# Two-layer graph network: summing each PSUM bank by itself, and a correction computed on GpSimd

## The reference

```python
# layer 0
h = jnp.maximum(_layernorm(x), 0.0)
mask = (adj > 0.0).astype(x.dtype)
W1a, W1b = W1[:F], W1[F:]                     # F = 64, H = 192
diff = h[:, :, None, :] - h[:, None, :, :]
hid = relu((h @ W1a)[:, :, None, :] + diff @ W1b + b1)
hm = jnp.einsum('bjkh,bjk->bjh', hid, mask)
x = x + hm @ W2 + deg[..., None] * b2
# layer 1
h = jnp.maximum(_layernorm(x), 0.0)
x = x + jnp.einsum('bno,fo->bnf', jnp.einsum('bnm,bmf->bnf', adj, h), W)
```

## Time and profile before

| | |
|---|---|
| median of three runs | 945.11 us (942.63 to 945.84) |
| the profiled execution, its own time | 940.0 us |
| its span, first to last instruction | 938.2 us |
| granted TensorE clock, mean | 0.989 |
| busy: PE, DVE, ACT, POOL | 889.5, 885.7, 832.2, 582.1 us |
| matmuls, DVE, ACT, POOL instructions | 9138, 3032, 1856, 1420 |

### The profile page before, as it was taken

The page is one execution under the profiler, slowest core; times in us unless marked ns, Lnnn a source line. Parts: engine busy times, 40 slices in busy tenths (PEclk is TensorE's granted clock), DMA queues, the critical chain, the costliest instruction groups (busy, mean ns, idle before and its releaser), DMA issues.

```text
span 938.2 us, 28102 instructions
## 1 busy us (share of the span) xinstructions
PE 889.5 (95%) x9138; PEld 818.6 (87%) x9139; DVE 885.7 (94%) x3032; ACT 832.2 (89%) x1856; POOL 582.1 (62%) x1420
## 2 busy tenths in 40 slices
PE   3879999999999999999999999999999999999996
PEld 1459999999999999999999999999999999999995
DVE  6999999999999999999999999999999999999993
ACT  3978999999999999999999999999999999899993
POOL 0856666666666665666666665666666666656664
PEclk9799999999999999999999999999999999999998
DMA  9500000000000000000000000000000000000000
GB/s 340 223 1 2 7 8 2 8 8 7 8 7 8 7 2 8 7 7 8 8 7 2 8 8 6 9 8 6 2 7 8 7 8 9 7 5 4 8 7 15
DMA packets 8114, 19.18 MB, mean 20 GB/s; under 512 B 1312, under 2 KB 5920, under 8 KB 6944
## 3 DMA queue, kind: packets, MB, share of 16 engines
q1 hardware_dynamic: 7056, 16.98, 4.8%
q10 hardware_dynamic: 912, 0.39, 0.2%
HBM read 13.17 MB, written 4.19 MB: 19 GB/s over the span
## 4 chain that ended last, share of the span: by engine, by line
PE 64%; DVE 25%; ACT 4%; issue 4%; POOL 1%; DMA 1%; DVEq 0%; SPq 0%; ACTq 0%; POOLq 0%
PE ring L353 31%; DVE acc L745 13%; PE post L438 8%; PE ring L379 5%; DVE onehot_space L729 5%; PE post L439 4%; ACT ring L502 3%; PE prep L409 3%; PE post L442 2%; PE prep L419 2%; PE prep L416 2%; PE prep L415 2%; DVE onehot_row L781 2%; DVE owner L775 1%; DMA x_all<-x_nbf_dram 1%
## 5 line engine op out<-in xcount | busy, mean ns | idle before, releaser
L502 ACT COPY ring<-P 128x768 f32<-128x768 f32 x512 | 405.2, 814 | 44.0 <-DVE acc L745 35.1
L353 PE MATMUL ring<-PQ,onehot_space 128*128 128x192 f16 x4096 | 401.0, 246 | 18.1 <-ACT ring L502 14.6
L353 PEld LDWEIGHTS ring<-PQ,onehot_space 128*128 128x128 f16 x4096 | 341.1, 99 | 29.8 <-DVE onehot_space L729 17.1
L745 DVE SCALAR_TENSOR_TENSOR acc<-ring,acc 128x768 f32<-128x768 f32 x384 | 362.2, 943 | 0.7 <-PE ring L353 0.7
L828 POOL TENSOR_TENSOR relu_row<-relu_row 128x192 f32<-128x192 f32 x256 | 154.4, 603 | 255.5 <-ACT relu_row L538 245.5
L729 DVE TENSOR_SCALAR onehot_space<-mask_all 128x256 f16<-128x256 f16 x1024 | 230.4, 266 | 0.0
L438 PE MATMUL post<-consts,acc 128*128 128x128 f32 x1024 | 154.4, 273 | 1.5 <-POOL relu_row L828 1.5
L745 DVE SCALAR_TENSOR_TENSOR acc<-ring,start 128x768 f32<-128x768 f32 x128 | 121.7, 951 | 28.3 <-PE ring L353 28.1
L438 PEld LDWEIGHTS post<-consts,acc 128*128 128x128 f32 x1024 | 114.2, 141 | 1.6 <-issue 1.6
L439 PE MATMUL post<-ownerT,relu_row 128*128 128x128 f32 x512 | 99.0, 275 | 0.0
L379 PE MATMUL ring<-PQ,owner 128*128 128x384 f16 (+1 forms) x512 | 93.9, 306 | 0.0
(11 more groups left out here) (129 smaller groups left out, 1609.1 us busy)
## 6 DMA issues: line engine op xcount, KB each, us to landing
adj_all<-adj_kbj_dram SPq DMA_DIRECT2D x8, 1024.0 KB, 17.9
x_all<-x_nbf_dram SPq DMA_DIRECT2D x8, 512.0 KB, 18.6
out_dram<-x_all SPq DMA_DIRECT2D x32, 128.0 KB, 1.7
consts<-consts_dram SPq DMA_DIRECT2D x1, 192.0 KB, 2.6
onehot_space<-w1a_dram ACTq DMA_DIRECT2D x2, 48.0 KB, 4.2
onehot_space<-w1b_dram ACTq DMA_DIRECT2D x2, 48.0 KB, 6.9
onehot_space<-b_dram ACTq DMA_DIRECT2D x1, 96.0 KB, 9.8
w2a<-w_dram ACTq DMA_DIRECT2D x1, 32.0 KB, 11.3
```

Source lines behind the costliest of these rows:

```text
L353: last = nc.tensor.matmul(to, hot(s), parts[:, part, H:2 * H], start=False, stop=(part == 1), skip_group_check=True)
L502: return nc.scalar.copy(slots[to], src.unsqueeze(1).unsqueeze(1).broadcast_to([N, BANKS, PER_BANK, H]))
L745: return nc.vector.scalar_tensor_tensor(sums, slots[to], 0.0, so_far, ALU.max, ALU.subtract if first else ALU.add)
```

## The change

Each sum instruction takes one PSUM bank (384 columns), so that both banks are added into one running sum of two slots (384 columns) and only two slots for each half k have to be transposed: 4 transposes a graph instead of 8. PE signals after each bank's gather (9 signals a graph instead of 5). DVE runs 8 half sums instead of 4 sums; the second half of a chunk waits for the first, and the second of two compares moves between the two halves. The correction `start` is no longer halved, and POOL makes it from the copy of P in SBUF, behind `p_ready` and the graph's first sum, in front of L851; ACT no longer makes it. What waited for `start_ready` to know that ACT had read `pq_ps` now waits for `p_ready`. (The kernel has a second form of the loop for graphs whose extra rows don't fit; its changes are left out here.)

```diff
-        acc_space = sb("acc", [N, 2, BANKS * ROW + N - H2])
-        acc = acc_space[:, :, 0:BANKS * ROW].rearrange("p g (a w) -> p g a w", a=BANKS)
+        acc_space = sb("acc", [N, 2, ROW + N - H2])
+        acc = acc_space[:, :, 0:ROW].rearrange("p g (s h) -> p g s h", h=H)
...
-                            dst = [slot(place(u, i), s) for s in range(SLOTS)]
                             hot = lambda s: onehot[:, hot_place(u // 2, i), s, u % 2, :]
                             pe.wait_ge(seeded, b * REGULAR + i + 1)
+                            for bank_ in range(BANKS):
+                                dst = [(s, slot(place(u, i), s)) for s in range(PER_BANK * bank_, PER_BANK * (bank_ + 1))]
+                                gather(dst, parts, hot).then_inc(gathered, 1)
...
                             for k in range(2):
-                                for s in range(SLOTS):
+                                for s in range(PER_BANK):
                                     hm = acc_space[:, (u + 1) % 2, s * H + k * N:s * H + (k + 1) * N]
                                     nc.tensor.matmul(sums_T_ps[:, k, :], hm, ident, start=(s == 0), stop=False, is_transpose=True)
...
-            def start_sums(b):
-
-                nc.scalar.activation(start[:, 0, :], pq_ps[:, 0:H], ACT.Relu, scale=spare[:, bass.ds(b, 1)]).then_inc(start_ready, 1)
...
-            def prepare(b, u, i):
+            def prepare(b, u, i, s):
...
-            def consume(u, to, first):
-
-                sums = acc[:, u % 2].rearrange("p a (s h) -> p a s h", h=H)
-                so_far = start[:, :, :].unsqueeze(1).broadcast_to([N, BANKS, PER_BANK, H]) if first else sums
-                return nc.vector.scalar_tensor_tensor(sums, slots[to], 0.0, so_far, ALU.max, ALU.subtract if first else ALU.add)
+            def consume(u, to, bank_, first):
+
+                sums = acc[:, u % 2]
+                return nc.vector.scalar_tensor_tensor(sums, slots[to][:, bank_], 0.0, start[:, :, :] if first else sums, ALU.max,
+                                                      ALU.subtract if first else ALU.add)
...
                     if i < REGULAR:
-                        prepare(b, u, i)
+                        prepare(b, u, i, 0)
                     if i == 3 and main and exists(b + 1):
-                        dve.wait_ge(start_ready, b + 2)
+                        dve.wait_ge(p_ready, b + 2)
                         second_part(b + 1, u + 1)
...
-                        dve.wait_ge(gathered, b * CHUNKS + i + 1)
-                        consume(u, place(u, i), i == 0).then_inc(summed, 1)
+                        dve.wait_ge(gathered, b * GATHERS + i * BANKS + 1)
+                        consume(u, place(u, i), 0, i == 0).then_inc(half_summed, 1)
+                    if i < REGULAR:
+                        prepare(b, u, i, 1)
+                    if main and i < REGULAR:
+                        dve.wait_ge(half_summed, b * REGULAR + i + 1)
+                        dve.wait_ge(gathered, b * GATHERS + i * BANKS + 2)
+                        consume(u, place(u, i), 1, False).then_inc(summed, 1)
...
+            def start_sums(b, u):
+
+                if isinstance(b, int):
+                    nc.gpsimd.tensor_scalar(start[:, 0, :], P[:, u % 2, :], spare[:, b:b + 1], 0.0, ALU.mult, ALU.max).then_inc(start_ready, 1)
...
                     pool.wait_ge(p_ready, b + 2)
+                    if exists(b):
+                        pool.wait_ge(summed, b * REGULAR + 1)
+                        start_sums(b + 1, u + 1)
                     nc.gpsimd.tensor_tensor(PQ[:, (u + 1) % 2, 1, 0:H], P[:, (u + 1) % 2, :], PQ[:, (u + 1) % 2, 0, 0:H],
                                             ALU.subtract).then_inc(p_part_ready, 1)
...
+            pool.wait_ge(p_ready, 1)
+            start_sums(0, 0)
             graphs(nc.gpsimd, step, some)
```

More of the change, by code:

```diff
@@ L42 @@
 CHUNKS = REGULAR + 1
+GATHERS = REGULAR * BANKS + 1
 COVERED = REGULAR * SLOTS
@@ L204, in gnn_kernel @@
         start_ready = sem("start_ready")
+        product_ready = sem("product_ready")
         onehot_ready = sem("onehot_ready")
@@ L212, in gnn_kernel @@
         gathered = sem("gathered")
+        half_summed = sem("half_summed")
         summed = sem("summed")
@@ L218, in gnn_kernel @@
         loop_gathered = sem("loop_gathered")
+        loop_half_summed = sem("loop_half_summed")
         loop_summed = sem("loop_summed")
@@ L350, in gather @@
             def gather(dst, parts, hot):
-                for s, to in enumerate(dst):
+                for s, to in dst:
                     for part in range(2):
@@ L373, in step @@
                             pe.wait_ge(summed, b * REGULAR + 2)
-                            dst = [row_slots[place(u, i)][:, s, :] for s in range(ROW_SLOTS)]
+                            dst = [(s, row_slots[place(u, i)][:, s, :]) for s in range(ROW_SLOTS)]
                             for bank_ in range(BANKS):
@@ L382, in step @@
                             pe.wait_ge(onehot_row_ready, b + 1)
-                            hot = lambda s: onehot_row[:, s, :]
-                        gather(dst, parts, hot).then_inc(gathered, 1)
+                            gather(dst, parts, lambda s: onehot_row[:, s, :]).then_inc(gathered, 1)
                     if i == 0 and main:
@@ L450, in step @@
                             pe.wait_ge(loop_seeded, first + k + 1)
-                            gather([slot(place(u, CHUNKS), s) for s in range(SLOTS)], parts, lambda s: onehot_row[:, s, :]).then_inc(loop_gathered, 1)
+                            gather([(s, slot(place(u, CHUNKS), s)) for s in range(SLOTS)], parts, lambda s: onehot_row[:, s, :]).then_inc(loop_gathered, 1)
             lead(step, hi=-1)
@@ L533, in step @@
                     if i == 1 and exists(b - 1):
-                        act.wait_ge(gathered, b * CHUNKS)
+                        act.wait_ge(gathered, b * GATHERS)
                         if exists(b - 2):
@@ L594, in _ @@
             act.wait_ge(tables_ready, 1)
-            act.wait_ge(pq_ready, 1)
-            start_sums(0)
             act.wait_ge(ring_ready, 1)
@@ L616, in _ @@
             nc.vector.memset(w3t[F:N, :], 0.0)
-            nc.vector.memset(acc_space[:, :, BANKS * ROW:], 0.0)
+            nc.vector.memset(acc_space[:, :, ROW:], 0.0)
             nc.vector.memset(start[:, :, :], 0.0).then_inc(loop_summed, 1)
@@ L717, in _ @@
             chain(nc.vector.scalar_tensor_tensor(spare[:, :], fits, float(SLOTS * LOOPED), spare[:, :], ALU.mult, ALU.add))
-            chain(nc.vector.tensor_scalar(spare[:, :], spare[:, :], -float(COVERED + SLOTS * LOOPED), -1.0 / BANKS, ALU.add, ALU.mult))
+            chain(nc.vector.tensor_scalar(spare[:, :], spare[:, :], -float(COVERED + SLOTS * LOOPED), -1.0, ALU.add, ALU.mult))
             nc.vector.tensor_scalar(loops[0:1, 1, :], fits[0:1, :], -float(LOOPED), float(LOOPED), ALU.mult, ALU.add)
@@ L730, in hot @@
                                                2.0 * (SLOTS * i + s) + 1.0, None, ALU.is_equal)
-            def prepare(b, u, i):
+            def prepare(b, u, i, s):
                 if i in HOT_AT[u % 2] and exists(b - u % 2 + 2):
                     k = u % 2 * REGULAR + HOT_AT[u % 2].index(i)
-                    for s in range(2):
-                        last = hot(b - u % 2 + 2, u - u % 2 + 2, k // 2, k % 2 * 2 + s)
-                        if k % 2 * 2 + s == SLOTS - 1:
-                            last.then_inc(onehot_ready, 1)
-            def consume(u, to, first):
-                sums = acc[:, u % 2].rearrange("p a (s h) -> p a s h", h=H)
-                so_far = start[:, :, :].unsqueeze(1).broadcast_to([N, BANKS, PER_BANK, H]) if first else sums
-                return nc.vector.scalar_tensor_tensor(sums, slots[to], 0.0, so_far, ALU.max, ALU.subtract if first else ALU.add)
+                    last = hot(b - u % 2 + 2, u - u % 2 + 2, k // 2, k % 2 * 2 + s)
+                    if k % 2 * 2 + s == SLOTS - 1:
+                        last.then_inc(onehot_ready, 1)
+            def consume(u, to, bank_, first):
+                sums = acc[:, u % 2]
+                return nc.vector.scalar_tensor_tensor(sums, slots[to][:, bank_], 0.0, start[:, :, :] if first else sums, ALU.max,
+                                                      ALU.subtract if first else ALU.add)
             def step(b, u, looped=False):
@@ L814, in step @@
                             dve.wait_ge(loop_gathered, first + k + 1)
-                            consume(u, place(u, CHUNKS), False).then_inc(loop_summed, 1)
+                            consume(u, place(u, CHUNKS), 0, False).then_inc(loop_half_summed, 1)
+                            wait_apart(dve, loop_half_summed, first + k + 1)
+                            consume(u, place(u, CHUNKS), 1, False).then_inc(loop_summed, 1)
             lead(step)
@@ L821, in _ @@
         def _(pool):
+            def start_sums(b, u):
+                if isinstance(b, int):
```

(6 more changed lines are left out.)

8 lines of the change are left out of this document (3 added, 5 removed).

## The result

The changed kernel takes 916.35 us (median of 4 runs, 915.53 to 916.97) against 944.41 for the kernel before beside it: ratio 0.9703, 95% interval 0.9684 to 0.9723. It is faster by 3%. The predicted time was 953, a little slower; 916.35 lies inside the range of 912 to 968, near the 914 of rival B. The executions of one kernel lie within about 1% of each other, except one of experiment 2 (1585.12) and the profiled one of experiment 3 (1024.96), which are compared with nothing.

The account below looks back on a forecast made before the run. Bounds: DVE's own stream, its 0.43 idle for PE in odd graphs, and DVE and POOL blocking each other. 127 x (6.835 - 6.783) = +6.6, start +1.8, end -0.4: 948.0 profiled, 953 on the median; range 912 to 968.

Parts of the forecast that it names:

- rival B: DVE's compares run through each time, no collision with POOL: mean 6.49 to 6.53 a graph, 914 on the median; 25%.
- POOL, the new instruction: Correction on POOL from Z + 4.24, taken as 0.62, pushing L851 to Z + 4.81 among DVE's three compares.
- collision of L851 with the three compares: POOL gets in between DVE's three L781 compares, holding one: 0.33 in even graphs, 0.36 in odd; 45%.
- Z: Time origin for each graph: the end of the fourth sum of the graph before.
- the four transposes: Four fewer on PE save 0.44 a graph; for the period this counts only as DVE's idle 0.43 in odd graphs.
- Halves: DVE's sums split in two: 0.466 each, 0.067 more than one sum, plus 0.11 waiting once a graph without a compare between.
- rival D: Each half sum on DVE pays its full length, 0.143 instead of 0.067: 0.30 a graph more, about 992; 5%.
- The hold on chunk 1's second compare: DVE compare held by POOL's add L828, 0.43 each graph; moved behind the first half sum, it is held no more.
- The period: Even graph 6.41 and odd 6.57 without collision; 6.74 and 6.93 with it, mean 6.835 against 6.783.
- The start: Graph 0's correction stands behind POOL's pow, 0.85 after it and done at 58.65: all graphs 1.8 later (0.9 to 2.4).
- Rival E: POOL's pow L844 holds the compare starting at Z + 3.53: 0.25 more, mean near 7.1, about 985; 5%.
- the end: After the last graphs, two sets of four transposes less on a waiting chain: -0.4.

Follow-up runs that it names:

- experiment 2: Changed kernel with a separate running sum for each bank and 8 transposes, so second halves do not wait for the first: 921.40, ratio 0.9755.
- experiment 3: The kernel of experiment 2 with both compares of a chunk ahead of its first half sum, as in the kernel before: 959.43, ratio 1.024.
- experiment 5: Changed kernel with the correction on ACT again, half sums, 4 transposes and moved compares kept: 931.29, ratio 0.986.
- experiment 4: Changed kernel with the correction as one two-input multiply, its relu left out, taking 0.50: 975.18, ratio 1.0323.
- experiment 8: Kernel before with only the correction moved to POOL, whole sums and 8 transposes kept: 948.74, ratio 1.0106.
- experiment 1: Kernel before with only 4 of the 8 transposes, two of the four slots left out of the result: 925.12, ratio 0.9802.
- experiment 9: Changed kernel with graph 0's correction on ACT, the later ones on POOL: 914.36, ratio 0.9736, beside 916.92 for the changed kernel run again.
- experiment 7: Changed kernel with POOL's L869 put ahead of the correction, there numbered L866: 924.54, ratio 0.9844.

## Why the prediction was wrong, step by step

**The step that failed** is "POOL, the new instruction", whose collision of L851 with the three compares (0.33 and 0.36 a graph) was the whole forecast of a slower kernel; the three compares were undisturbed instead, 182 ns each in the mean. The correction was put at 0.62 between bounds of 0.38 and 0.70, and took 0.94, above both. At the start of the kernel it takes 0.93 while DVE stands idle (58.17), so its length is its own and no contention. The bounds came from one-input operations of 64 columns with an immediate and from two-input adds; a one-input operation of 192 columns with a pointer to a number for each partition and two arithmetic steps was not among the rows. With 0.94, L869 begins at Z + 5.28 to 5.38 instead of Z + 4.81, and the three compares, at Z + 4.72 to 4.82 (predicted 4.73), are over by Z + 5.2. The prediction had named that case, "if the correction is so long that L851 begins after them", but given it no weight in the range of the length.

**The length alone would not have mended it:** the correction itself, running under the three compares, was taken as able to hold the first of them ("up to 0.46 if the correction runs long"). By the prediction's rule that whoever holds the way makes the other wait, a correction of 0.94 would have held the first compare until near its own end, about as long as the forecast collision. It holds only in its first 0.29, and the compares come 0.36 behind its start. And it keeps the two-input operations L869 and L876 away from them: with the correction gone they are held 0.19 (experiment 5), with a short one 0.55 (experiment 4). The correction was costed as a burden at this place; it is a shield there, worth 15 us (931.29 less 916.35), while in the kernel before, whose compares stood elsewhere, it costs 1% (experiment 8). With the bias multiply in its one-input form there is nothing to shield from, and the kernel is faster without the correction on POOL (911.80).

**What held, and what else was off:**
- PE: the four transposes removed nothing but DVE's idle time before odd graphs' first sums (experiment 1).
- Halves: 0.466 each, and 0.11 of waiting where nothing stands between them. The sum with rival D's 0.143 a half is out: it gave 992.
- The rule of the Trainium skill (VectorE: DVE Perf Modes, the section on the TRN2 errata), by which each of many small instructions pays a fixed latency, gave an estimate of 982; this case's distances of 0.47 between a half and what follows it don't agree, nor does the measured time.
- The hold on chunk 1's second compare is won back: 0.21 both times in the trace.
- The period: in the odd graph the compares of chunk 1 start at Z + 2.06 and Z + 2.66, as predicted. The prediction's 6.41 and 6.57 without a collision became 6.51 and 6.63. The 0.10 in the even graph comes in at its head, where a pair of compares takes 0.49 instead of 0.35 (465.67) beside POOL's later last operations (L774 gives some of it back, 0.22 instead of the 0.33 expected); 0.05 of the odd one's 0.06 is the compare at 477.89, 0.26 instead of 0.21, beside L876. Rival B had 0.04 for the mean of 6.49; 0.08 came (6.566).
- The start: 2.3 late for 1.8, which experiment 9 gives back. From the pow's end to the correction 1.0 instead of 0.85 (57.17 to 58.17), and the correction 0.93 instead of 0.62.
- Rival E: the compare at 469.10 takes 0.21 while the pow L859 runs; it isn't held. The pow is the one that gets longer: 0.57 in the five graphs in which no L726 compare starts inside it, as for L844 before, and 0.69 to 0.74 in the 123 in which one does.
- Of the end, -0.4 was predicted and +1.0 came. 0.6 of it lies in the last graph's own sums, whose halves have no compares between them: from the first sum to the residual add behind the fourth 5.03 (893.04 to 898.07) against 4.44 (918.24 to 922.68).

**By the sum:** predicted 127 x 0.052 + 1.8 - 0.4 = +8.0; measured 127 x (-0.217) + 2.3 + 1.0 = -24.3. The period makes up all of the error: 0.27 a graph, the 0.345 of the collision that didn't come, less the 0.08 that POOL's later work took.

**Luck:** rival B had the right sign and the right path, no hold on the three compares, but for another reason, that DVE wins. That its 914 comes within 3 us is in part luck: for the profiled execution it had 909.3, and 916.14 came. The factor of 1.0054 from the profiled execution to the median, read from the kernel before, added 5; the changed kernel has none (916.14 and 916.35).

**Open:** why the correction takes 0.94, and why it holds compares for 0.29 of that only; why POOL gets in when it starts up to 0.08 behind the first compare and waits for the whole series from 0.09 on (experiment 8); how the 38 us of experiment 3 are made up; and the other 0.4 at the end.

## What to carry to other kernels

When two engines hold each other up, cost a moved or added operation by what it pushes and what it lets through: the same correction cost 1% in one schedule (experiment 8) and saved 1.6% in another (experiment 5 against the changed kernel). Take its length from a row of its own form (number of tensor inputs, pointer or immediate, columns), and where none exists, let the range of its length run on until the order of what follows changes. And PE's saving, with PE busy for 95% of the span, was worth here the wait that it removed from DVE and what that moved behind it (0.125 a graph), and not its own 0.44.

## What the runs showed of the hardware

- POOL operations with one tensor input hold DVE's compares in their first part only: L830 (192 columns, 0.94) until 0.29 after its start, in 114 graphs of two traces; started at 468.01 in experiment 7, where it takes 1.00, until 0.34; L872 (64 columns, 0.54) by 0.04 at 460.52. A compare that comes later runs beside them undisturbed. Operations with two tensor inputs hold them until 0.13 before their own recorded end: L876 (485.34 against 485.21), L871 (463.72 against 463.59), L866 (461.49 against 461.36). The pow L859, two inputs but one column, doesn't (469.10), and is itself 0.13 longer. The Trainium skill (SBUF — State Buffer, section "SBUF: two separate sides") says of DVE and GpSimd that of a GpSimd operation and a DVE one that uses two ports or has two SBUF inputs, whichever starts first has the shared pair of ports for the whole instruction and the other fully blocks. For two-input POOL operations of many columns the rows agree but for the last 0.13; for the one-input ones they don't.
- A series of compares that has begun is not broken into by a POOL operation that starts 0.09 to 0.16 behind its first compare; POOL waits for all three, or all five (L857 0.64, or 0.90 instead of 0.55). One that starts at most 0.08 behind gets in (experiments 4 and 8).
- One tensor input is slower than two on POOL here: 0.94 against 0.50 for 192 columns (a pointer and two arithmetic steps against one multiply), 0.52 against 0.29 for 64 columns (one multiply each; 0.45 in the two graphs in which no compare runs beside it). The Trainium skill (GPSIMD Engine Reference, section "Engine selection") has it the other way: two inputs about twice as slow as VectorE, one input roughly at full rate. These rows don't agree with it.
- A half sum that waits for the one directly ahead of it starts 0.58 after it, against 0.466 by its columns: 0.11 for the wait. Without the wait (experiment 2) two halves take 1.01 instead of 1.13.
